# Non-local attention with stacked fp16 scores, sums by products with ones, and the second pass of one query group beside the first pass of the next

## The reference

```
xf    = x.reshape(8, 64, 1024)
theta = w_theta @ xf            # (8, 32, 1024)
phi   = w_phi   @ xf
g     = w_g     @ xf
attn  = softmax(theta^T phi, over the last axis m)     # (8, 1024, 1024)
y     = sum over m of attn[n, m] * g[:, m]             # (8, 32, 1024)
x     = w_last @ y + x
```

## Time and profile before

| | us |
|---|---|
| median of 3 runs | 1356.36 |
| lowest and highest of them | 1351.65, 1360.01 |
| the profiled execution, its own time | 1351.59 |
| its span, from the first to the last instruction | 1349.8 |
| non-local stage, start and end within the span | 10.1, 201.1 |

### The profile page before, as it was taken

The page is one execution under the profiler, slowest core; times in us unless marked ns, Lnnn a source line. Parts: engine busy times, 40 slices in busy tenths (PEclk is TensorE's granted clock), DMA queues, the critical chain, the costliest instruction groups (busy, mean ns, idle before and its releaser), DMA issues. The chain is left out here.

```text
span 1349.8 us, 29364 instructions
## 1 busy us (share of the span) xinstructions
PE 1227.4 (91%) x12618; PEld 830.9 (62%) x12618; DVE 604.3 (45%) x1006; ACT 625.5 (46%) x1191; POOL 191.0 (14%) x207
## 2 busy tenths in 40 slices
PE   8998989888888698899879999999999999988876
PEld 5433328777777577778755665555566556566454
DVE  3992124112111466677743344333434434355672
ACT  2997754323567544344443443334343434343361
POOL 4100003960000332122222000100100000003000
PEclk9558999999999899899979999999999999999998
DMA  5900000000000033311150000000000000032002
GB/s 116 128 1 1 1 1 5 1 1 1 1 1 1 25 83 87 89 52 45 31 137 5 12 5 1 9 9 1 1 9 8 1 1 1 1 63 64 1 0 63
DMA packets 63613, 35.91 MB, mean 27 GB/s; under 512 B 31325, under 2 KB 62109, under 8 KB 63485
## 3 DMA queue, kind: packets, MB, share of 16 engines
q1 hardware_dynamic: 63101, 32.98, 11.2%
q10 hardware_dynamic: 384, 1.07, 0.3%
HBM read 22.37 MB, written 2.21 MB: 18 GB/s over the span
## 5 line engine op out<-in xcount | busy, mean ns | idle before, releaser
L1317 DVE TENSOR_TENSOR sp_sums<-sp_y,sp_shared 64x512 f32<-64x512 f32 (+1 forms) x256 | 176.3, 689 | 263.0 <-ACT sp_shared L1292 237.3
L1288 ACT COPY sp_sums<-sp_y 64x512 f32<-64x512 f32 x256 | 148.8, 581 | 240.7 <-PE sp_y L1183 235.9
L1183 PE MATMUL sp_y<-hankel,sp_ut 128*128 128x256 f16 x768 | 125.7, 273 | 0.0
L1250 PE MATMUL sp_o<-sp_sums,mix 128*64 128x128 f32 (+2 forms) x1024 | 122.8, 390 | 0.0
L1169 PE MATMUL sp_y<-hankel_sum,sp_ut 128*128 128x512 f16 x384 | 104.9, 383 | 0.0
L1169 PE MATMUL sp_y<-hankel,sp_ut 128*128 128x512 f16 x384 | 104.5, 381 | 0.3 <-ACT sp_sums L1288 0.3
L1180 PE MATMUL sp_y<-hankel,sp_late 128*128 128x256 f16 x512 | 98.0, 273 | 0.0
L503 PE MATMUL convv<-runningv,toeplitz 128*128 128x128 f32 x610 | 83.7, 284 | 12.6 <-DVE runningv L523 12.6
L503 PE MATMUL convh<-runningh,toeplitz 128*128 128x128 f32 x610 | 84.0, 283 | 8.1 <-DVE runningh L523 8.1
L1180 PEld LDWEIGHTS sp_y<-hankel,sp_late 128*128 128x128 f16 x512 | 48.4, 98 | 64.5 <-issue 18.8
L1250 PEld LDWEIGHTS sp_o<-sp_sums,mix 128*64 128x64 f32 x1024 | 64.0, 134 | 38.2 <-issue 27.5
(11 more groups left out here) (344 smaller groups left out, 2097.8 us busy)
## 6 DMA issues: line engine op xcount, KB each, us to landing
hankel<-phi_rows SPq DMA_DIRECT2D x32, 160.0 KB
hankel_sum<-phi_rows SPq DMA_DIRECT2D x32, 128.0 KB, 3.3
win_xt<-normed SPq DMA_DIRECT2D x64, 56.0 KB, 2.4
ex_w<-in_L_ffn_weight SPq DMA_DIRECT2D x1, 2080.0 KB
m_plus<-in_L_ffn_M_phi_plus SPq DMA_DIRECT2D x2, 1024.0 KB, 13.7
m_minus<-in_L_ffn_M_phi_minus SPq DMA_DIRECT2D x2, 1024.0 KB, 16.4
sp_late<-sp_ut SPq DMA_DIRECT2D x32, 64.0 KB, 2.1
out<-x SPq DMA_DIRECT2D x8, 256.0 KB, 3.8
```

The lines of the kernel that those rows point to most:

```text
L1183: mm = nc.tensor.matmul(out[:, :, P:SPAN], ut[g % 2][:, hu, b, s, :, :].rearrange("p a c -> p (a c)"), m.hankel[:, hf, some, P:SPAN], star ...
L1250: mm = nc.tensor.matmul(out_of(lo, cnt, par), m.mix[:, 2 * j + n, SCALES - 1 - seg, par, :], sums[:, n, :, lo + par:lo + cnt:2], start=Fal ...
L1288: nc.scalar.copy(sums[HALF[a], :, b, to], y_ps[r][HALF[a], :, of]).then_inc(y_c[r], 1)
L1317: nc.vector.tensor_tensor(sums[HALF[a], :, b, to], y_ps[r][HALF[a], :, of], shared[done % 2][HALF[a], :, of], op).then_inc(y_c[r], 1)
```

## The change

The stage is written anew; everything outside it stays. What it does:

- theta and phi are made per image as three copies of 32 rows (96 partitions). ScalarE writes the fp16 rounding of all three, VectorE then replaces one of the three by the remainder (value less rounding), a different one for theta and phi. One fp16 product 96 rows deep so gives high x high + low x high + high x low. To keep fp16 in range the projection matrices are first divided by a bound on theta and phi, worked out from the largest absolute values of x and of the weights (`size_w`, `size_x`, `fac`), and the exponential multiplies the bound back in (`scale=fac[:, 4:5]`).
- The three pieces of the negative maximum become three more rows of theta (partitions 96 to 98) against rows of phi that hold 2^15; so the shift is part of the same product, 99 rows deep. ScalarE copies them there, four copies for each group.
- The first pass takes only maxima. The sums come from TensorE: `attend` has four more products, of ones with the probabilities, into a PSUM tile beside the values; VectorE takes their reciprocal (128x512) and multiplies.
- First-pass work is cut into 40 "lane" pairs of two images each: 8 pairs that make theta or phi, 32 pairs of row blocks, each row block 128x1024 in one of two PSUM slots. 13 pairs (`AHEAD`) run before the second pass starts; the others are handed out within the units, two in units 0, 2, 4 and 6, one in the other units up to 22, none after.
- The second pass keeps its 32 units. The ring has two banks of 512 columns, one for each image's scores, and shift, scores and outputs take their turns in it. ScalarE's exponentials are of 512 columns.
- POOL's copies with swapped halves go; it clears rows of phi and other buffers instead.

```diff
+    lane = (made_pairs(0) + rows_pairs(0, 0) + made_pairs(1) + rows_pairs(0, 1)
+            + rows_pairs(1, 0) + made_pairs(2) + rows_pairs(1, 1) + made_pairs(3)
+            + rows_pairs(2, 2) + rows_pairs(2, 3) + rows_pairs(3, 2) + rows_pairs(3, 3))
+    AHEAD = last_of[0] + 2
+    lane_end = [AHEAD]
+    for u in range(UNITS):
+        lane_end.append(min(len(lane), lane_end[-1] + (2 if u < NB and u % 2 == 0 else 1)))
+    for u in range(UNITS):
+        w = u // NB
+        if u % NB == 0:
+            ring_order.append(("shift", w, 0))
+        ring_order += [("probs", u, 0), ("probs", u, 1)]
+        if u % NB == 1 and w:
+            ring_order += [("out", w - 1, 0), ("out", w - 1, 1)]
+        ring_order += [("probs", u, 2), ("probs", u, 3)]
...
-        ps = [pb(f"nl_ps{k}", [P, T]) for k in range(4)]
-        ring = [ps[2], ps[0], ps[1]]
-        y_ps, o_ps = ps[3][:, 0:BANK], ps[3][:, BANK:T]
+        slot = [pb(f"nl_slot{k}", [P, T]) for k in range(2)]
+        ring_ps = pb("nl_ring", [P, T])
+        both_ps = pb("nl_heads", [P, T])
+        y_ps, sum_ps = both_ps[:, 0:BANK], both_ps[:, BANK:T]
...
             @block.tensor
+                def lane_pair(n):
+                    kind, h, w, kk = lane[n]
+                    if kind == "rows":
+                        k = (w % NH) * PER + kk
+                        for p, im in enumerate(images(n)):
+                            pe.wait_ge(slot_done, 2 * n + p - 1)
+                            for c in range(NH):
+                                mm = nc.tensor.matmul(slot[p][:, c * BANK:(c + 1) * BANK], theta[0:WIDE, im, k * P:(k + 1) * P],
+                                                      phi[0:WIDE, im, c * BANK:(c + 1) * BANK], start=True, stop=True)
+                            mm.then_inc(s_ok, 1)
+                    else:
+                        if n:
+                            pe.wait_ge(slot_done, 2 * n)
                         for c in range(NH):
+                            for p in range(2):
+                                mm = nc.tensor.matmul(slot[p][0:WIDE, c * BANK:(c + 1) * BANK], proj[HALF[p], int(kind == "phi"), :],
+                                                      m.x[HALF[p], h, c * BANK:(c + 1) * BANK], start=True, stop=True)
+                                if c == NH - 1:
+                                    mm.then_inc(q_ok, 1)
...
+                def score_t(u, i):
+                    w, k = u // NB, u % NB
+                    im, c = (w // NH) * QUAD + i, w % NH
+                    out = take_ring(("probs", u, i))
+                    if k == 0:
+                        pe.wait_ge(turn_c, QUAD * w + i + 1)
+                    nc.tensor.matmul(out, phi[0:WIDE + CUTS, im, k * P:(k + 1) * P], theta[0:WIDE + CUTS, im, c * BANK:(c + 1) * BANK],
+                                     start=True, stop=True).then_inc(t_ok, 1)
 
                 def attend(u):
+                    pe.wait_ge(p_ok, QUAD * (u + 1))
+                    if k == 0 and w:
+                        pe.wait_ge(y_c, w)
+                    for i in range(QUAD):
+                        nc.tensor.matmul(y_ps[rows_of(i), :], vt[:, k, q * QUAD + i, :], probs_t[u % 2][:, i, :], start=(k == 0), stop=(k == NB - 1))
+                    for i in range(QUAD):
+                        mm = nc.tensor.matmul(sum_ps[rows_of(i), :], ones[:, 0:CB], probs_t[u % 2][:, i, :], start=(k == 0), stop=(k == NB - 1))
                     mm.then_inc(a_ok, 1)
...
+                values(0)
+                pe.wait_ge(diag_x_ok, 1)
+                nc.tensor.matmul(slot[0][:, BANK:BANK + P], ones[:, :], diag_x[:, :], start=True, stop=True).then_inc(big_x, 1)
+                pe.wait_ge(lt_c, QUAD)
+                values(1)
+                pe.wait_ge(scaled_ok, 6)
+                for n in range(AHEAD):
+                    lane_pair(n)
+                pe.wait_ge(v_c, 2)
                 for u in range(UNITS):
+                    if u % NB == 0:
+                        turn_shift(w)
+                    score_t(u, 0)
+                    score_t(u, 1)
+                    if u:
+                        attend(u - 1)
+                    if u % NB == 1 and w:
+                        output(w - 1, 0)
+                        output(w - 1, 1)
+                    score_t(u, 2)
+                    score_t(u, 3)
+                    for n in range(lane_end[u], lane_end[u + 1]):
+                        lane_pair(n)
+                attend(UNITS - 1)
...
             @block.scalar
+                def high_pieces(n):
+                    if lane[n][0] != "rows":
+                        into = theta if lane[n][0] == "theta" else phi
+                        for p, im in enumerate(images(n)):
+                            act.wait_ge(q_ok, made_before[n] + p + 1)
+                            nc.scalar.copy(into[0:WIDE, im, :], slot[p][0:WIDE, :]).then_inc(hi_ok, 1)
...
+                for u in range(UNITS):
+                    if u % NB == 0:
+                        act.wait_ge(turn_ok, w + 1)
+                        for i in range(QUAD):
+                            nc.scalar.copy(theta[WIDE:WIDE + CUTS, (w // NH) * QUAD + i, c * BANK:(c + 1) * BANK], out[i * CB:i * CB + CUTS, :]).then_inc(turn_c, 1)
+                    for i in range(QUAD):
+                        act.wait_ge(t_ok, QUAD * u + i + 1)
+                        nc.scalar.activation(probs_t[u % 2][:, i, :], ring(("probs", u, i)), ACT.Exp, scale=fac[:, 4:5]).then_inc(p_ok, 1)
+                    for n in range(lane_end[u], lane_end[u + 1]):
+                        high_pieces(n)
...
             @block.vector
+                    step(nc.vector.tensor_reduce(size_x[:, q:q + 1], m.x[:, 2 * q:2 * q + 2, :].rearrange("p g n -> p (g n)"), axis=AX.X, op=ALU.max, apply_absolute_value=True))
...
+                def lane_pair(n):
+                        if kind == "rows":
+                            nc.vector.tensor_reduce(nmax[:, w, kk, i:i + 1], slot[p][:, :], axis=AX.X, op=ALU.max, negate=True).then_inc(slot_done, 1)
+                        else:
+                            into, low = (theta, slice(CB, 2 * CB)) if kind == "theta" else (phi, slice(2 * CB, 3 * CB))
+                            nc.vector.tensor_tensor(into[low, im, :], slot[p][low, :], into[low, im, :], ALU.subtract).then_inc(slot_done, 1)
+                    if n in last_of:
+                        cut(last_of.index(n))
 
                 def take_heads(w):
                     dve.wait_ge(a_ok, NB * (w + 1))
+                    nc.vector.reciprocal(inv[:, :], sum_ps).then_inc(inv_ok, 1)
+                    dve.wait_ge(inv_ok, w + 1)
+                    nc.vector.tensor_tensor(heads[w % 2][:, :], y_ps, inv[:, :], ALU.mult).then_inc(y_c, 1)
...
+                for u in range(UNITS):
+                    if u % NB == 0 and w:
+                        take_heads(w - 1)
+                    if u % NB == 1 and w:
+                        add(w - 1, 0)
+                        add(w - 1, 1)
+                    for n in range(lane_end[u], lane_end[u + 1]):
+                        lane_pair(n)
```

More of the change, by code:

```diff
@@ L151, in rows_of, with ring, images @@
             return slice(im * CB, (im + 1) * CB)
-        def slots(s):
-            n = s + 1 if s else 0
-            return ps[2 * (n % 2)], ps[2 * (n % 2) + 1]
-        TURN_AT = {2: 0, 6: 1}
-        SCALE_AT = 4
+        def ring(use):
+            k = ring_at[use] % 2
+            return ring_ps[:, k * BANK:(k + 1) * BANK]
+        def images(n):
+            return 2 * lane[n][1], 2 * lane[n][1] + 1
         with nc.Block() as block:
@@ new lines, in take_ring @@
+                def take_ring(use):
+                    n = ring_at[use]
+                    if n >= 2:
+                        kind, a, b = ring_order[n - 2]
+                        if kind == "probs":
+                            pe.wait_ge(p_ok, QUAD * a + b + 1)
+                        elif kind == "shift":
+                            pe.wait_ge(turn_c, QUAD * (a + 1))
+                        else:
+                            pe.wait_ge(o_c, 2 * a + b + 1)
+                    return ring(use)
@@ new lines, in turn_shift @@
+                def turn_shift(w):
+                    pe.wait_ge(cut_ok, w + 1)
+                    out = take_ring(("shift", w, 0))
+                    for kk in range(PER):
+                        mm = nc.tensor.matmul(out[:, kk * P:(kk + 1) * P], pieces[:, w, kk, :, :].rearrange("p i c -> p (i c)"), ident16[:, :], start=True, stop=True)
+                    mm.then_inc(turn_ok, 1)
+                def score_t(u, i):
[6 more added lines that the diff above has]
+                                     start=True, stop=True).then_inc(t_ok, 1)
@@ L334, in _ @@
+                attend(UNITS - 1)
+                output(NW - 1, 0)
+                output(NW - 1, 1)
             @block.scalar
@@ L357, in _ @@
-                for j in range(2 * UNITS):
-                    u, pair = j // 2, j % 2
```

(30 more changed lines are left out.)

366 lines of the change are left out of this document (121 added, 245 removed).

## The result

The changed kernel takes 1421.8 us (median of 4 runs, 1418.11 to 1425.01) against 1356.86 (4 runs, 1351.65 to 1360.01): a ratio of 1.0484, 95% interval [1.0447, 1.0521]. The direction was forecast, the size was not: 1396 had been given, and 1421.8 lies 1.8 us above the top of the range (1420), with single runs on both sides of that bound.

What follows compares the result with a forecast made beforehand. VectorE's maxima were taken to bound the first pass, TensorE the second. Stage terms 66.0 + 119.4 + 4.8 + 14 + 21 + 11 = 236.2 us against 200.75, plus 7 for clock, gave 1394, stated as median 1396; range 1368 to 1420.

Steps and rivals of the forecast that it cites:

- Start: Stage start up to the first lane pair: small VectorE instructions, maxima of x, second values; 20.7 us, bounds 19.3 and 23.
- Both cost nothing: Claim that SP's weight loads and POOL's larger clearing of phi, done long before the cut at 61 us, add no time.
- The clock term: Half clock for two made pairs and the first 7 us of the second pass: 7 us, bounds 0 and 16.
- the boundaries: Three group changes in the second pass: shift copies, reciprocal in the path, outputs; 7.0 us each, 21 together.
- signs of being wrong: Unit near 3 us, reciprocal under 1, stage end before 215, or a clock row of 0.5 between 75 and 225 us.
- The unit: Second-pass period of 3.85 us, with or without a lane pair, set by the chain through ScalarE; 31 make 119.4 us.
- the tail: After the last unit: exponential, `attend`, reciprocal, multiplication, two outputs and additions; 11 us.
- lanes and first shift: Before the second pass: 13 lane pairs and the cut 41.8 us, then shift copies and first exponential 3.5, to 66.0.
- The first: Rival: TensorE never waits in the second pass, units cost 3.6 or 2.7 us; 1346 us, 7 in 100.
- The second: Rival: half clock through the second pass, 6.9 us a unit; 1482 us, 4 in 100.
- The third: Rival: maxima not hidden, each of 25 lane pairs adds its 2.3 us; 1451 us, 3 in 100.
- the changes of tiling mode: Every unit switches to 32-column tiles and back; by the drain rule 0.16 us more per unit, 5 us in sum.

Runs made afterwards that it cites:

- Run 1: Changed kernel with GpSimd's clearings and copies started only after VectorE has scaled the projections, nothing left out: 1414.44 us, 1.0457 of the kernel before.
- run 9: Changed kernel with GpSimd's work later and unread TensorE products behind the first values and lane pairs, none before the first lane pair: 1407.01 us, 1.0402.
- Run 2: Changed kernel with unread identity products keeping TensorE at work, six before the first lane pair and more behind each: 1414.21 us, 1.0465.
- runs 3: Changed kernel with the reciprocal of the sums replaced by a copy, so the result is multiplied by the sums: 1407.81 us, 1.0415.
- run 12: run 9 and run 10 combined, reciprocal cut into two of 256 columns in the next group's units 1 and 2, multiplication and outputs later: 1403.1 us, 1.033.
- run 7: Changed kernel with all 40 lane pairs ahead of the second pass and none in its units: 1483.15 us, 1.0955.
- run 5: Changed kernel with each unit's products with ones moved behind the next unit's third and fourth score products: 1425.44 us, 1.0531.
- run 4: Changed kernel with the products with ones left out in 28 of 32 units, so the sums are wrong: 1404.95 us, 1.038.
- run 10: Changed kernel with sums and heads copied out of PSUM, reciprocal and multiplication made from the copies, outputs one unit later: 1424.72 us, 1.054.
- run 8: Changed kernel with GpSimd late, unread products also before the first lane pair, sums moved, double made pairs taken apart: 1410.37 us, 1.0436.

## Why the prediction was wrong in size and right in sign

**The step that failed is "Start".** Its price for VectorE's twelve small instructions, 3.1 us, was that of instructions with nothing beside them, and the sentence on POOL's clearing ("Both cost nothing") looked only at when the cleared buffers are needed. It counted POOL's 7.5 us from 31.9 us on; from 10.1 to 31.9 us of the same trace POOL is busy for 10.58 us. Run 1 took the work away and VectorE was done at 19.05 us, where 19.3 was forecast; with it, it is done at 29.4. Counted from the stage's first instruction, the lanes start at 20.2 us in the changed kernel, at 13.1 in run 1 and at 11.0 in run 9, where the second values run at full clock too; the forecast has 10.6. So GpSimd's work cost 7.1 us here and the half clock behind it 2.1. The Trainium skill, "SBUF — State Buffer", section Who interferes with whom, states the rule: VectorE and GpSimd share a pair of SBUF ports that one instruction holds to its end, casts and `tensor_scalar` can ask for it, `tensor_reduce` never does. The trace agrees: the stalled ones end with POOL's instructions, and L393, beside the clearing, takes 2.29 us, as the two of run 1 without it (4.60 together).

**The clock term was mis-sized**: 7 us, where the trace shows about 16. The projection products of the four made pairs ahead take 3.36 to 3.73 us instead of 1.96, 6.2 more in all; unit 0 takes most of another 3.2, and the boundaries an estimated 6.6 of their 7.3. Run 2 gives back 6.2 us at the stage's end, run 9 with the start 16.3. The forecast had seen the cause (TensorE idle, then half clock) and given it to two of four made pairs and to one place of the second pass, although it had itself put an idle gap at every boundary. No run takes the clock alone out of a boundary: runs 3 and 12 shorten the gap and bring them to 6.2 to 6.8 us, below the forecast's 7.0, but change the work there too.

**The range** was too narrow upward for the same two reasons. It allowed 2 us for the start, 9 for the clock and nothing upward for the boundaries, and took it that these rarely add. No term came out below its price, and the lanes, unit 0 and the boundaries share the clock as a cause, so they did add. One of the signs of being wrong that it names came, too: PEclk 0.50 from 85 to 90 us.

**What held.** The unit (3.85, measured 3.92), the same with and without a row pair (run 7), bound by the chain through ScalarE (run 5); the sums at 0.85 us (run 4); the reciprocal by 6.4 ns a column (3.36 us for 512; 1.75 for 256 in run 12); units 2, 4 and 6; the tail; lanes and first shift once the clock is full (run 9).

**The rivals.** The first needed a unit at 3.6 or 2.7 us. It came out at 3.92 with a row pair and without, as the chain is not hidden; where run 5 opens the chain, TensorE's own work comes to 3.93 and 3.07. The second falls: plain units are at 1.00. The third falls by run 7; its 25 lane pairs should have been 27, of which 23 are row pairs. On the changes of tiling mode, run 5 adds two a unit and shows 0.10 us more for the values, 0.10 for the score products between and 0.03 for the sums, 0.23 us for the two. The plain unit itself came out 0.07 us longer than forecast, not 0.16, which fits that TensorE has 0.22 us to spare in it. The Trainium skill, "TensorEngine Tiling (Array Packing)", section Tiling Modes, says that such a change drains TensorE. The trace agrees in direction.

**Where the gain went.** 48 of the 64 maxima did leave the path, and the second pass starts 27 us earlier. But a unit costs 3.92 us instead of 2.37, which is 50 us over 32 units: 27 of it for the sums, which ScalarE used to make beside the maxima; the other 22 were not taken apart. Boundaries and double units add 52 us, where the old pass had 13.5 (89.3 less 32 x 2.37) for everything but its units.

## What to carry to other kernels

Moving a bottleneck engine's work beside another stage pays only what that stage has idle: price the new beat of that stage first, times its count. Before a small VectorE copy or scaling is priced, look at what GpSimd does at that moment; and work moved off one engine's path goes where the next queue has slack, in pieces of about that slack (run 12 against run 10: 1.75 us into 1.57). A chain that leaves TensorE idle can be paid twice, for the wait and for the half clock behind it (3.38 instead of 1.86 us for the `attend` behind the first boundary), and products that nobody reads help only where TensorE would wait anyway (run 9 against run 8).

## What was not expected of the hardware

- A `TENSOR_SCALAR` of two columns took 3.07 us beside a clearing by GpSimd and 0.23 without; one of a single column took 0.20 beside GpSimd's copies.
- At the first boundary the granted clock falls twice: PEclk is 0.50 from 138.1 to 141.4 us, behind waits of 0.75 and 1.34 us for the copies of the shift, and again from 144.9 to 148.2, from the end of the wait of 1.99 us for the heads on. It is 1.00 from 160 to 170, where the units follow one another.
- A reciprocal of 128x512 takes 3.36 us where a copy of the same shape takes 0.69.
